# Gates' operations, low parts of the rotary weights and value weights moved in a fused attention and expert kernel

## The chip, the cores and the metric

The kernel runs on one core of a Trainium2 chip, as one program. The metric is the time of one execution on the device in microseconds, the lower the better. Five engines run their own instruction streams and meet at semaphores: PE (matrix products), DVE (VectorE), ACT (ScalarE), POOL (GpSimd) and SP, which here only issues DMA transfers. The rows call TensorE's weight loads PEld and the queues in which an engine issues transfers SPq and ACTq.

## The reference

A transformer block with modulation from a condition vector, attention with low-rank queries, keys and values and rotary parts, and a routed mixture of experts. Inputs: x of 4 x 512 x 256, 16 heads.

```
mod = (silu(c) @ wmod)                       # sa, ca, ga, sb, cb, gb
ga = (2*(ga >= 0) - 1) * max(|ga|, 0.25)      # the gates
gb = (2*(gb >= 0) - 1) * max(|gb|, 0.25)
h  = layernorm(x) * (1 + ca) + sa
c_q, c_kv = rmsnorm(h @ Wq_down), rmsnorm(h @ Wkv_down)
q, k, v   = c_q @ Wq_up, c_kv @ Wk_up, c_kv @ Wv_up
q_rope, k_rope = rope(h @ Wq_rope), rope(h @ Wk_rope)
attn = softmax((q k^T + q_rope k_rope^T) * scale)
x = x + ga * (attn @ v) @ Wout
h = layernorm(x) * (1 + cb) + sb
x = x + gb * (experts(h) + shared(h))         # 16 experts, 4 of them for each token
```

## The kernel before, in words

Float32 products are made of three: every operand is split in a high and a low part (`wr_hi`/`wr_lo`, `qk[..., 0/1, :]`, `mout[:, 0/1]`), and `mm3` (lines 677 to 679) multiplies high by high, high by low and low by high. ScalarE writes the high part, VectorE subtracts it from the source for the low part, and TensorE waits for both.

The work has four stages: inputs and latents, a passage up to attention, the attention loop, the experts. The change touches the second and the third.

The attention loop has 256 units: a head of a batch is four units, one for each tile of 128 keys, a pair of heads is eight, a batch 64. In unit u TensorE weighs values (`weigh_values`, line 857), forms the scores of unit u + 3 (`score`), the products for the maximum of unit u + 9 (`score_max`, line 834) and what `AUX_AT[u]` lists: rotary rows of a pair (`pr`), latent rows (`kl`), turned outputs (`ot`, line 811), the output product (`op`). ScalarE takes two exponentials for each unit (lines 1631, 1634), GpSimd the low part `p_lo` (line 1896), `rotate` (line 1874) and `add_rows`. VectorE's list in a unit is fixed: `turn` (lines 1216, 1217), `low_outputs`, `gated`, `row_max` (line 1243, nine units ahead, two PSUM banks), then `safe_gate` in units 4 to 19, `low_rows` (line 1223), and in every fourth unit `normalise` (lines 1250, 1253). Each engine works through its own list in order.

`safe_gate(b, step)` (lines 1262 to 1268) makes ga and gb of batch b from the raw gates in `gate[:, b + 1]`, 128 x 512 floats, in four chained operations. Its scratch is `y_gate`, where `gated` later writes the product of gates and output.

`shift_row(s)` on SP (line 560) copies a head's four rows of maxima to row 0 of `qk` for the scores of that head; `pad_slots(b)` on ScalarE's queue (line 1674) writes constant rows to the `slots` in HBM, 2880 KB for a batch, at unit 12 of the batch.

Ahead of the loop: line 1190 makes `wr_lo`, the low part of all rotary weights, 8 pairs of heads, in one VectorE operation of 4096 elements, and `wr_l` tells it. It stands between `norm_latents(0)` and `split_latents(0)`, `squares(1)`. `squares(1)` feeds GpSimd's `inverse_norms(1)` (line 1859, `rms`), that `norm_latents(1)` (lines 1137, 1139). Then come the turns of pair 1 behind the fills of `rows_f` (SP, lines 537 and 543), four low rows, the value weights `mout` (TensorE line 870, ScalarE 1692, VectorE 1201, two PSUM banks used in turn, four quarters), eight maxima, and the turns of pair 2. The raw gates are TensorE products (`row_modulations`, line 757, two banks in turn) that ScalarE copies (`row_gates`, line 1592). `wr_raw` and the value weights' source `wout_s` lie in the memory of `qk`, whose first writers wait for that reason on `wr_l` and `m_mm`.

The functions that the diff touches, and what calls them:

Of the kernel before, what the change touches and what calls it, by code (L numbers as in the profile page):

```python
# [39 lines left out]
TB = SEQ // P  # L40
# [83 lines left out]
GATES_AT = 4  # L124
# [13 lines left out]
def program(nc, x, cT, wmod, wdn, wqup, wkup, wvup, wout, wrope, trig, eye, qnw_bc, kvw, kvw2, wgate, w13, w2,  # L138
            route, out):
    ctx = ExitStack()  # L140
    with ctx:
# [141 lines left out]
        gabs, gsgn = (y_gate[:, n].rearrange("p q d -> p (q d)") for n in range(2))  # L283
# [214 lines left out]
        def _(sp):  # L498
# [47 lines left out]
            def fill_latents(s):  # L546

                b = s // H
                if s < RING:
                    sp.wait_ge(*((m_mm, 4) if s >= 2 else (wr_l, 1)))  # L550
                else:
                    sp.wait_ge(s_score, TB * (s - RING + 1))
                sp.dma_start(qk[SPARE:RD, s % RING, 0].bitcast(F32), lat_st[KL:LATENTS, b % 2].bitcast(F32))\
                    .then_inc(q_lat[s % RING], 16)
# [120 lines left out]
        def _(pe):  # L675
# [186 lines left out]
            def value_weights():  # L862
                pe.wait_ge(ld_v, 48)
                pe.wait_ge(p_dnev, NB)
                for q in range(4):
                    if q >= 2:
                        pe.wait_ge(m_ev, q - 1)
                    for pr in range(2 * q, 2 * q + 2):
                        for s in range(2):
                            mm = pe.matmul(out_bank[q % 2][s * KL:(s + 1) * KL, (pr % 2) * D:(pr % 2 + 1) * D],  # L870
                                           wvup_s[:, 2 * pr + s, :], wout_s[:, 2 * pr + s, :], start=True, stop=True)
                    mm.then_inc(m_mm, 1)
# [16 lines left out]
            row_modulations(1)  # L889
            aux(("kl", 1))  # L890
            value_weights()
            row_modulations(2)
            pe.wait_ge(p_clo, NB)
            pe.wait_ge(spared, 2)
            for k in range(TB):
                score_max(k)
            row_modulations(3)
            for k in range(TB, 2 * TB):
                score_max(k)
# [181 lines left out]
        def _(dve):  # L1081
# [82 lines left out]
            def up_weights():  # L1164
                dve.wait_ge(ld_c, 16 * 4)
                for z in range(2):
# [22 lines left out]
            dve.wait_ge(wr_h, 1)  # L1189
            dve.tensor_tensor(wr_lo[:].rearrange("p k g n -> p (k g n)"), wr_raw,  # L1190
                              wr_hi[:].bitcast(F32).rearrange("p k g n -> p (k g n)"), ALU.subtract).then_inc(wr_l, 1)
# [3 lines left out]
            def value_weights():  # L1195

                for q in range(4):
# [59 lines left out]
            def safe_gate(b, step):  # L1257

                g = gate[:, b + 1].rearrange("p w n -> p (w n)")
                if step == 0:  # L1260
                    dve.wait_ge(g_ev, b + 1)
                    dve.tensor_scalar(gsgn, g, 0.0, 0.5, ALU.is_ge, ALU.subtract)
                elif step == 1:
                    chain(dve.scalar_tensor_tensor(out=gabs, in0=g, scalar=-1.0, in1=g, op0=ALU.mult, op1=ALU.max))
                elif step == 2:
                    chain(dve.tensor_scalar(gabs, gabs, 0.25, 2.0, ALU.max, ALU.mult))
                else:
                    chain(dve.tensor_tensor(g, gabs, gsgn, ALU.mult))
# [4 lines left out]
            split_latents(1)  # L1273
            split_latents(2)
# [3 lines left out]
            for s in range(2):  # L1278
                low_rows(s, 1)
                low_rows(s, 0)  # L1280
            value_weights()
# [25 lines left out]
            for u in range(UNITS):  # L1307
# [10 lines left out]
                if GATES_AT <= u < GATES_AT + 4 * NB:  # L1318
                    safe_gate((u - GATES_AT) // 4, (u - GATES_AT) % 4)
# [252 lines left out]
        def _(act):  # L1572
# [111 lines left out]
            act.wait_ge(wr_l, 1)  # L1684
# [5 lines left out]
            for q in range(4):  # L1690
                act.wait_ge(m_mm, q + 1)
                act.activation(mout[:, 0, 2 * q:2 * q + 2, :], out_bank[q % 2][:].rearrange("p (a n) -> p a n", a=2),
                               ACT.Copy, scale=kvw2_s[:, 0:1]).then_inc(m_h, 1)
            row_gates(2)
            row_gates(3)
# [127 lines left out]
        def _(pool):  # L1823
# [80 lines left out]
            pool.wait_ge(wr_l, 1)  # L1904
# [151 lines left out]
```

## Time and profile before

| | us |
|---|---|
| median of 3 runs | 1024.6 (1023.91 to 1026.63) |
| profiled execution | 1026.2 |
| its span | 1024.4 |
| PE busy | 876.5 (86%) |
| DVE busy | 733.5 (72%) |
| POOL busy | 675.8 (66%) |
| ACT busy | 573.9 (56%) |
| TensorE clock granted, mean | 0.927 of full |

Busy time is the sum over instructions and overlaps a little where an engine pipelines. A stretch in which one engine is busy all the time is bound by it; elsewhere the waits have to be read. The span is that of the profiled execution, and the rows date everything from its start.

### The profile page before, as it was taken

The page shows a single profiled execution, that of the slowest core. Times are in us where ns is not written, and L with a number is a line of the kernel's source. Part 1 is how long each engine was busy: PE and PEld are TensorE (multiplying, and loading weights), DVE is VectorE, ACT ScalarE, POOL GpSimd, SP SyncE. Part 2 cuts the span into 40 slices and gives each one's busy share as a digit, 9 for nine tenths or more (in the row PEclk, how much of TensorE's full clock was granted, in tenths as well). Part 3 has the DMA queues.
Part 4 walks back from the last instruction along what each step waited for, and adds up shares of the span by engine and source line. Part 5 has one row for each costly group of instructions (what it writes and reads, how often), then busy time and mean ns, then how long its engine had stood idle before and what let it go on. Part 6 is the DMA issues. An engine that isn't in the chain of part 4 may idle for free.

```text
span 1024.4 us, 19916 instructions
## 1 busy us (share of the span) xinstructions
PE 876.5 (86%) x6996; PEld 744.5 (73%) x6996; DVE 733.5 (72%) x1596; ACT 573.9 (56%) x1071; POOL 675.8 (66%) x641
## 2 busy tenths in 40 slices
PE   5678889999999999999999988449974999999920
PEld 5546568888878888788887877438853899999910
DVE  5766997878887788786879775664843566666656
ACT  1335667788787877887787876422310444444400
POOL 3664667888888788887887975505675355555544
PEclk9889989999999999999999998858996899999965
DMA  7561421333523235232325253323222333333264
GB/s 289 195 155 34 148 44 40 81 79 80 155 44 85 55 85 174 48 81 48 85 54 155 48 205 113 100 51 114 88 106 107 109 115 122 116 120 119 82 236 174
DMA packets 65757, 111.20 MB, mean 109 GB/s; under 512 B 16918, under 2 KB 43293, under 8 KB 63821
## 3 DMA queue, kind: packets, MB, share of 16 engines
q1 hardware_dynamic: 46905, 69.24, 25.3%
q10 hardware_dynamic: 11843, 22.84, 6.3%
q0 software_dynamic: 6912, 17.84, 4.5%
q8 instruction: 59, 0.97, 0.4%
q14 instruction: 38, 0.30, 0.1%
HBM read 46.06 MB, written 39.58 MB: 84 GB/s over the span
## 4 chain that ended last, share of the span: by engine, by line
PE 60%; DVE 12%; DMA 9%; POOL 9%; issue 6%; ACT 3%; SPq 0%; POOLq 0%; DVEq 0%; ACTq 0%
PE bank L677 13%; PE bank L679 11%; PE bank L678 11%; PE bank L857 7%; DMA slots<-h,slot_i 7%; PE bank L1072 7%; PE bank L834 4%; POOL p_lo L1896 3%; POOL slots L1951 2%; PE bank L1044 2%; PE bank L931 2%; DVE nmax L1243 2%; POOL turns L1874 1%; DVE turns L1216 1%; POOL h_hl L1852 1%
## 5 line engine op out<-in xcount | busy, mean ns | idle before, releaser
L1896 POOL TENSOR_TENSOR p_lo<-p_f,p_hi 128x512 f16<-128x512 f32 x256 | 326.4, 1286 | 57.3 <-ACT p_f L1634 56.8
L1243 DVE TENSOR_REDUCE nmax<-bank 128x1 fp32r<-128x512 f32 x256 | 174.6, 686 | 96.2 <-PE bank L834 92.6
L1631 ACT ACTIVATE p_hi<-bank,log_up 128x512 f16<-128x512 f32 x256 | 176.2, 688 | 114.4 <-PE bank L679 105.5
L1634 ACT ACTIVATE p_f<-bank,log_up 128x512 f32<-128x512 f32 x256 | 175.3, 685 | 11.3 <-POOL p_lo L1896 11.3
L857 PEld LDWEIGHTS bank<-vals,p_hi 128*128 128x128 f16 x2048 | 111.1, 98 | 54.2 <-issue 27.0
L857 PE MATMUL bank<-vals,p_hi 128*128 128x66 f16 x2048 | 139.6, 195 | 10.1 <-POOL p_lo L1896 9.6
L1874 POOL TENSOR_TENSOR turns<-turns 128x512 f32<-128x512 f32 x64 | 90.8, 1420 | 66.9 <-DVE turns L1217 66.9
L1223 DVE TENSOR_TENSOR qk<-rows_f,qk 128x512 fp32r<-128x512 f32 (+1 forms) x128 | 131.9, 1030 | 2.2
L677 PE MATMUL bank<-qk 128*128 128x512 f32 x256 | 123.4, 482 | 11.1 <-issue 10.2
L857 PE MATMUL bank<-vals,p_lo 128*128 128x66 f16 x1024 | 121.8, 194 | 0.0
L834 PE MATMUL bank<-qk 128*128 128x512 f32 x256 | 104.6, 410 | 3.7 <-DVE nmax L1243 3.6
L1951 POOL DMA_INDIRECT slots<-h,slot_i x64 | 66.1, 1033 | 57.9 <-DMA slots<-h,slot_i 24.5
L679 PE MATMUL bank<-qk 128*128 128x512 f32 x256 | 103.3, 404 | 0.0
L678 PE MATMUL bank<-qk 128*128 128x512 f32 x256 | 101.8, 398 | 0.0
L857 PEld LDWEIGHTS bank<-vals,p_lo 128*128 128x128 f16 x1024 | 96.8, 97 | 0.5
L834 PEld LDWEIGHTS bank<-qk 128*128 128x128 f32 x256 | 79.3, 310 | 17.9 <-DVE nmax L1243 6.8
L1964 POOL DMA_INDIRECT parts<-h,sel_i x80 | 79.8, 997 | 13.2 <-POOL idle L1963 11.9
L1072 PE MATMUL bank<-w_p,gT 88*128 x320 | 82.2, 379 | 0.0
L1623 ACT ACTIVATE qk<-rows_f 128x512 fp32r<-128x512 f32 (+1 forms) x128 | 80.6, 629 | 1.9 <-DMA rows_f<-turns 0.3
L1963 POOL TENSOR_TENSOR idle<-mhalf 128x1 f32<-128x1 f32 x80 | 14.9, 186 | 83.6 <-ACT h L1817 83.5
L1817 ACT ACTIVATE h<-bank 128x256 f32<-128x256 f32 x80 | 30.8, 385 | 61.3 <-PE bank L1072 61.3
L1528 DVE TENSOR_TENSOR x_hl<-bank,x_hl 128x256 fp32r<-128x256 f32 x80 | 34.0, 425 | 40.3 <-ACT x_hl L1804 40.0
(229 smaller groups left out, 2133.2 us busy)
## 6 DMA issues: line engine op xcount, KB each, us to landing
rows_f<-turns SPq DMA_DIRECT2D x64, 256.0 KB, 3.9
slots<-pad ACTq DMA_DIRECT2D x4, 2880.0 KB, 10.1
h<-slots SPq DMA_DIRECT2D x80, 144.0 KB
w_hi<-parts SPq DMA_DIRECT2D x16, 512.0 KB, 8.5
rows_f<-kl_f SPq DMA_DIRECT2D x32, 192.0 KB, 3.0
w_raw<-in_w ACTq DMA_DIRECT2D x4, 1408.0 KB, 11.8
h_dram<-h_hl SPq DMA_DIRECT2D x3, 1024.0 KB, 3.9
qk<-lat_st SPq DMA_DIRECT2D x16, 192.0 KB, 4.0
```

What stands on the lines that cost most here:

```text
L677: pe.matmul(dst, l_hi, r_hi, start=start, stop=False)
L678: pe.matmul(dst, l_hi, r_lo, start=False, stop=False)
L679: return pe.matmul(dst, l_lo, r_hi, start=False, stop=stop)
L834: pe.matmul(max_bank[q % 2][:], qk[:, s % RING, 0, 0, :].rearrange("k (p t) -> k t p", t=TB)[:, q, :], qk[:, s % RING, 1, 0, :], start=Tru ...
L857: mm = pe.matmul(out_bank[s % 2][:, q * VW:(q + 1) * VW], p[:, c, tok], vals[:, s // H * TB + c, a, :], start=(c == 0 and q == 0 and n == ...
L1072: mm = pe.matmul(y_bank[j % 2][:, 0:D], gT[:, j % 2, 0, h, :], w2_s[:, bass.ds(expert, 1), h, :].rearrange("p a n -> p (a n)"), start=(h = ...
L1223: dve.tensor_tensor(qk[rows, s % RING, x, 1, :], rows_f[rows, (s // 2) % 2, x, s % 2, :], qk[rows, s % RING, x, 0, :].bitcast(F32), ALU.su ...
L1243: dve.tensor_reduce(nmax[:, k % MAXES:k % MAXES + 1], max_bank[q % 2][:], AX_X, ALU.max, negate=True)\
L1631: act.activation(p_hi[:, u % TB, :], score_bank[u % 2][:], ACT.Exp, bias=log_up[:, 0:1], scale=SCALE)
L1634: act.activation(p_f[:, u % 2, :], score_bank[u % 2][:], ACT.Exp, bias=log_up[:, 0:1], scale=SCALE)\
L1874: pool.tensor_tensor(turns[:, 0, w], turns[:, 0, w], turns[:, 1, w], ALU.add if w else ALU.subtract).then_inc(s_eo, 1)
L1896: pool.tensor_tensor(p_lo[:, u % TB, :], p_f[:, u % 2, :], p_hi[:, u % TB, :], ALU.subtract).then_inc(s_pl, 1)
```

## The change

The gates' sixteen steps leave units 4 to 19 for units 4, 7, 10, ..., 49. Their scratch becomes `small` (`gate[:, 0]`) and the four operations are others: max(-g, g); max with 0.25; (g >= 0) times that; twice that less the magnitude. `wr_lo` is made in two goes: pairs 0 and 1 where all of it was made, pairs 2 to 7 behind `split_latents(1)`; `wr_l` counts to 2. Those that need only pairs 0 and 1 wait for 1, the others for 2. The value weights go in two halves, on TensorE with the products for the gates of batch 3 between them and those of batch 2 before `kl` of pair 1, on VectorE each half ahead of a head's low rows. The maxima follow in one row. ScalarE copies the gates of batch 2 ahead of `high_rows` and those of batch 3 between the halves.

```diff
-GATES_AT = 4
...
-        gabs, gsgn = (y_gate[:, n].rearrange("p q d -> p (q d)") for n in range(2))
...
-                    sp.wait_ge(*((m_mm, 4) if s >= 2 else (wr_l, 1)))
+                    sp.wait_ge(*((m_mm, 4) if s >= 2 else (wr_l, 2)))
...
-            def value_weights():
+            def value_weights(half):
                 pe.wait_ge(ld_v, 48)
                 pe.wait_ge(p_dnev, NB)
-                for q in range(4):
+                for q in (2 * half, 2 * half + 1):
                     if q >= 2:
                         pe.wait_ge(m_ev, q - 1)
...
             row_modulations(1)
+            row_modulations(2)
             aux(("kl", 1))
-            value_weights()
-            row_modulations(2)
+            value_weights(0)
+            row_modulations(3)
+            value_weights(1)
             pe.wait_ge(p_clo, NB)
             pe.wait_ge(spared, 2)
-            for k in range(TB):
+            for k in range(2 * TB):
                 score_max(k)
-            row_modulations(3)
-            for k in range(TB, 2 * TB):
-                score_max(k)
+            pe.wait_ge(wr_l, 2)
             aux(("pr", 0, 2))
...
-            dve.wait_ge(wr_h, 1)
-            dve.tensor_tensor(wr_lo[:].rearrange("p k g n -> p (k g n)"), wr_raw,
-                              wr_hi[:].bitcast(F32).rearrange("p k g n -> p (k g n)"), ALU.subtract).then_inc(wr_l, 1)
+            def low_rotary(at):
+                dve.wait_ge(wr_h, 1)
+                dve.tensor_tensor(wr_lo[:, :, at], wr_raw.rearrange("p (k g n) -> p k g n", k=KD, g=PAIRS)[:, :, at],
+                                  wr_hi[:, :, at].bitcast(F32), ALU.subtract).then_inc(wr_l, 1)
+
+            low_rotary(slice(0, 2))
             split_latents(0)
             squares(1)
...
                 if step == 0:
                     dve.wait_ge(g_ev, b + 1)
-                    dve.tensor_scalar(gsgn, g, 0.0, 0.5, ALU.is_ge, ALU.subtract)
+                    ins = dve.scalar_tensor_tensor(out=small, in0=g, scalar=-1.0, in1=g, op0=ALU.mult, op1=ALU.max)
                 elif step == 1:
-                    chain(dve.scalar_tensor_tensor(out=gabs, in0=g, scalar=-1.0, in1=g, op0=ALU.mult, op1=ALU.max))
+                    ins = dve.tensor_scalar(small, small, 0.25, None, ALU.max)
                 elif step == 2:
-                    chain(dve.tensor_scalar(gabs, gabs, 0.25, 2.0, ALU.max, ALU.mult))
+                    ins = dve.scalar_tensor_tensor(out=g, in0=g, scalar=0.0, in1=small, op0=ALU.is_ge, op1=ALU.mult)
                 else:
-                    chain(dve.tensor_tensor(g, gabs, gsgn, ALU.mult))
+                    ins = dve.scalar_tensor_tensor(out=g, in0=g, scalar=2.0, in1=small, op0=ALU.mult, op1=ALU.subtract)
+                chain(ins)
...
             split_latents(1)
+            low_rotary(slice(2, PAIRS))
             split_latents(2)
...
             for s in range(2):
+                value_weights(s)
                 low_rows(s, 1)
                 low_rows(s, 0)
-            value_weights()
...
-                if GATES_AT <= u < GATES_AT + 4 * NB:
-                    safe_gate((u - GATES_AT) // 4, (u - GATES_AT) % 4)
+                if u >= 4 and u % 3 == 1 and u // 3 <= 4 * NB:
+                    safe_gate((u // 3 - 1) // 4, (u // 3 - 1) % 4)
...
             row_gates(1)
-            act.wait_ge(wr_l, 1)
+            row_gates(2)
+            act.wait_ge(wr_l, 2)
...
             for q in range(4):
+                if q == 2:
+                    row_gates(3)
                 act.wait_ge(m_mm, q + 1)
...
-            row_gates(2)
-            row_gates(3)
...
             pool.wait_ge(wr_h, 1)
-            pool.wait_ge(wr_l, 1)
+            pool.wait_ge(wr_l, 2)
```

## Rows read from the trace of the kernel before

**Rows 1.** Timeline, VectorE, units 3, 19, 35, 51: start, duration, engine, line, operation.
```profile
102.98 0.42 DVE L1253 TENSOR_TENSOR o_tok<-bank,rinv 128x256 f32<-128x256 f32 x1
...
145.92 0.42 DVE L1253 TENSOR_TENSOR o_tok<-bank,rinv 128x256 f32<-128x256 f32 x1
...
180.69 0.42 DVE L1253 TENSOR_TENSOR o_tok<-bank,rinv 128x256 f32<-128x256 f32 x1
...
213.94 0.42 DVE L1253 TENSOR_TENSOR o_tok<-bank,rinv 128x256 f32<-128x256 f32 x1
```

**Rows 2.** Busy times by stretch: PE, PEld, DVE, ACT, POOL, clock, DMA share, GB/s.
```profile
103.00:145.90 42.90, 36.48 (x312) 27.77 (x311) 41.66 (x57) 29.38 (x48) 28.05 (x21) 0.92 0.36 104
...
123.60:135.30 11.70, 10.04 (x65) 8.06 (x65) 11.00 (x15) 6.38 (x11) 7.62 (x6) 0.71 0.40 115
...
164.20:197.40 33.20, 33.14 (x319) 27.63 (x318) 27.10 (x44) 26.62 (x44) 28.07 (x23) 1.00 0.30 77
```

**Rows 3.** Groups of VectorE by line, 103 to 146 us: busy us, mean ns.
```profile
L1262 DVE TENSOR_SCALAR y_gate<-gate 128x512 f32<-128x512 f32 x4 | 4.7, 1180 | 0.0
L1264 DVE SCALAR_TENSOR_TENSOR y_gate<-gate 128x512 f32<-128x512 f32 x4 | 3.5, 884 | 0.0
L1268 DVE TENSOR_TENSOR gate<-y_gate 128x512 f32<-128x512 f32 x4 | 3.1, 783 | 0.1
L1266 DVE TENSOR_SCALAR y_gate<-y_gate 128x512 f32<-128x512 f32 x4 | 2.8, 693 | 0.0
```

**Rows 4.** Timeline around TensorE's longest idle time in that stretch; in brackets idle time before.
```profile
117.13 0.40 ACTq L1674 DMA_DIRECT2D slots<-pad  x1
...
119.40 0.49 SPq L560 DMA_DIRECT2D qk<-nmax  x1
...
125.26 0.77 PE L677 MATMUL bank<-qk 128*128 128x512 f32 x1 [4.36 <-issue]
...
126.25 0.63 PE L679 MATMUL bank<-qk 128*128 128x512 f32 x1
```

**Rows 5.** Timeline: TensorE's first weighing of values.
```profile
92.04 0.19 PE L857 MATMUL bank<-vals,p_hi 128*128 128x66 f16 x1 [2.12 <-POOL p_lo L1896]
```

**Rows 6.** Timeline, TensorE: first and last product of an output group, a rotary product.
```profile
186.68 0.28 PE L677 MATMUL bank<-mout,oT 128*128 128x256 f32 x1
...
188.00 0.28 PE L679 MATMUL bank<-mout,oT 128*128 128x256 f32 x1
...
189.76 0.39 PE L678 MATMUL bank<-h_st,wr_hi 128*128 128x512 f32 x1
```

**Rows 7.** Timeline around the low part of the rotary weights, 33 to 54 us.
```profile
33.66 2.37 POOL L1852 TENSOR_TENSOR h_hl<-h_f,h_hl 128x1024 fp32r<-128x1024 f32 x1 [5.18 <-ACT h_hl L1579]
...
41.53 4.41 DVE L1190 TENSOR_TENSOR wr_lo<-qk_raw,wr_hi 128x4096 fp32r<-128x4096 f32 x1
...
42.19 7.61 POOL L1852 TENSOR_TENSOR h_hl<-h_f,h_hl 128x1024 fp32r<-128x1024 f32 x1 [2.64 <-ACT h_hl L1579]
...
50.42 2.90 POOL L1859 TENSOR_TENSOR rms<-ve,mhalf 128x16 f32<-128x16 f32 x1
```

**Rows 8.** Timeline from the turns of pair 1 to the maxima, 62 to 84 us.
```profile
62.47 0.69 DVE L1216 TENSOR_TENSOR turns<-bank,trig_s 128x512 f32<-128x512 f32 x1 [1.05 <-DMA rows_f<-turns]
62.55 2.59 ACT L1623 ACTIVATE qk<-rows_f 128x512 fp32r<-128x512 f32 x4 [0.29 <-DMA rows_f<-turns]
...
64.87 4.76 DVE L1223 TENSOR_TENSOR qk<-rows_f,qk 128x512 fp32r<-128x512 f32 x4
...
70.46 3.68 PE L870 MATMUL bank<-qk_raw,wvup_s 128*64 128x256 f32 x16 [3.80 <-DVE mout L1201]
...
77.17 2.70 DVE L1243 TENSOR_REDUCE nmax<-bank 128x1 fp32r<-128x512 f32 x4 [1.44 <-PE bank L834]
...
78.97 1.89 PE L757 MATMUL bank<-wmod_s,csil_bc 128*128 128x256 f32 x8
...
81.15 2.70 DVE L1243 TENSOR_REDUCE nmax<-bank 128x1 fp32r<-128x512 f32 x4 [1.28 <-PE bank L834]
```

More of the change, by code:

```diff
@@ L1188, in _, with value_weights @@
                 .then_inc(ab_l, 1)
-            dve.wait_ge(wr_h, 1)
-            dve.tensor_tensor(wr_lo[:].rearrange("p k g n -> p (k g n)"), wr_raw,
-                              wr_hi[:].bitcast(F32).rearrange("p k g n -> p (k g n)"), ALU.subtract).then_inc(wr_l, 1)
+            def low_rotary(at):
[3 more added lines that the diff above has]
+            low_rotary(slice(0, 2))
             split_latents(0)
             squares(1)
-            def value_weights():
-                for q in range(4):
+            def value_weights(half):
+                for q in (2 * half, 2 * half + 1):
                     dve.wait_ge(m_mm, q + 1)
```

## The prediction, made before the changed kernel was run

> **What bounds the kernel now.** I read the granted clock and busy times by stretch first, then the normalisation of each head as a clock of the attention loop, then the engines around its start.
>
> The loop runs 256 units. `normalise` runs once in four, so its rows date the units: unit 3 at 102.98, unit 19 at 145.92, unit 35 at 180.69, unit 51 at 213.94 [rows 1]. Sixteen units thus take 42.94 us, 34.77 and 33.25. In a 33.20 us stretch of the steady part PE is busy for 33.14 at clock 1.00, with DVE at 27.10 and POOL at 28.07 [rows 2]: PE sets the pace. In the first stretch it is DVE: busy 41.66 of 42.90 [rows 2]. What is there and not later is `safe_gate`, four operations for each of four batches in units 4 to 19: 4.7 + 3.5 + 3.1 + 2.8 = 14.1 us [rows 3]. PE also stands still there for 4.36 us, until 125.26: the score of head 4 needs the row of maxima that SP sent off at 119.40, 2.3 us after ScalarE had put the 2880 KB `pad` transfer on the DMA engines [rows 4].
>
> Ahead of the loop, up to the first weighing of values at 92.04 [rows 5], PE works in short bursts between waits; who ends each wait is the chain that I follow below.
>
> **Part 1, the gates.** Removed from units 4 to 19: 14.1 us of DVE. Put back: steps at units 4, 7, ... 49, of which six (4 to 19) stay in the first block, five come in units 20 to 35 and five up to 49. The forms change: three two-input operations and one single-operand one for each batch. Their prices are the rows' means, 884 and 783 ns for two inputs, 693 for the two-constant scalar form [rows 3]; I take 0.85 for each, so 5.1 us in the first block. DVE's other work in 16 units is 27.10 in the steady part [rows 2], less what the first block does not have yet: two `gated` and one `low_outputs`, 0.7 each by their size, so 25.0. DVE then needs 30.1 us. PE needs the steady 33.2 less the output products, which start at unit 23: two groups of twelve, from 186.68 to 188.00 plus one spacing of 0.12, 1.44 each [rows 6], and less one turn of outputs, 0.5: 29.8. Two engines at 29.8 and 30.1, coupled through two banks of maxima, do not run at the larger of the two: that is the lower bound. The upper is the old block less only the operations taken out, 42.94 - (14.1 - 5.1) = 33.9. I take 31.8, halfway, since the gate is now one unit in three and DVE can catch up between. Gain: 42.94 - 31.8 = 11.1 us (9.0 to 12.8, and 7 if the new steps are stretched by POOL to the rows' longest). The 4.36 us stall is inside it: if DVE no longer lags, row 4's maxima leave before the pad transfer. If it lags still, up to 4.4 of the 11.1 is lost.
>
> Units 20 to 35: five steps add 4.3 to 27.1, 31.4 under PE's 33.2. The block took 34.77, partly PE coming back from a low clock; I take 34.1, gain 0.6 (-1.0 to 1.5). Units 36 to 51: DVE 31.4 again, POOL 28.1 plus what the gates hold it up; PE goes on at 33.25 with small slips, -0.3 (-1.5 to 0). Nothing else reads the scratch (`small`) before unit 107. Sum of part 1: 11.4 us.
>
> POOL's p_lo shares something with DVE: POOL's subtraction of one input took 2.37 us beside no long DVE operation and 7.61 beside the rotary low part of 4.41 us [rows 7]. So each gate step may hold POOL for up to its own length: 5.3 x 0.7 = 3.7 on 28.07 in a block, 31.8 of 33.2.
> The Trainium skill (SBUF — State Buffer, "Who interferes with whom") says that a VectorE instruction with two SBUF inputs, or one in a two-port mode, and a GpSimd instruction that reads SBUF exclude each other for a whole instruction. The 7.61 agrees. By that rule all four new forms lock the pair, as all four old ones did, and spreading them moves the blocking into blocks where POOL also adds rows; that speaks against the change and is rival B below. The same section says that a GpSimd instruction which only writes SBUF is not held; no row here has the new overlap of that kind.
>
> **Part 2, the rotary low part in two goes.** The whole is 4096 elements in 4.41 us [rows 7]; a quarter, 1.1, now stands ahead of `split_latents(0)` and `squares(1)`, and 3.3 go behind `split_latents(1)`. So DVE reaches `squares(1)` 3.3 us earlier, though not before ScalarE's high part of the latents; POOL's subtraction (start 42.19) is free of the long operation and ends at 45 to 46.5 instead of 49.8; the power `rms` starts at 47.1 instead of 50.42 [rows 7]. Taken: 3.3 us (2.5 to 3.9), carried to `norm_latents(1)`, ScalarE's `kl_f`, SP's fills of `rows_f`, and the first of the DVE's turns of pair 1, 62.47 to 59.2 [rows 8]. The 3.3 us moved back fit where DVE stood idle: 2.9 us before the latents of batch 2 and 1.05 before that turn, the latter noted in its row [rows 8]. If they do not fit, 0.5 is lost. What now waits for both goes (SP's first latents, ScalarE's `high_rows`, POOL's zeroing and, behind it, rotate(1)) gets them at about 57.3, before its other inputs.
>
> **Part 3, the order ahead of attention.** In the old order DVE did all four low rows (64.87, 4.76 us) before the value weights, PE's third quarter of value weights could start only at 70.46 after 3.80 us idle, and the maxima came in two groups, 77.17 to 79.87 and 81.15 to 83.85, with the gates' products of batch 3 (1.89 us) between [rows 8]. New, by the same durations:
> ScalarE's `row_gates(2)` now stands ahead of `high_rows`. Its products follow PE's turn of the latents at 55.4 to 56.3 by two groups of 1.89, so end at 60.0; the copy ends at 60.7, which is 1.5 later than the fills: a new wait, with four `high_rows` (2.59), `key_latents(1)` and two copies of value weights queued behind it. These end at 63.3, 63.9, 64.6 and 65.2. DVE, done with its turns at 61.7, waits for them, does two low parts to 66.0 and low rows of head 0 to 67.5. PE does the first half of the value weights at 61.3 to 63.2, the products of batch 3 to 65.1, and the second half to 67.2 by 0.66 us after each bank is free. ScalarE's copies end at 67.9, DVE's low parts at 68.9, low rows of head 1 at 70.4. Eight maxima in one chain, 0.60 to 0.65 each, end at 75.4 instead of 83.85: 8.45 us earlier. From there to 92.04 the order is the old one (scaled values' low part, turns of pair 2, POOL's rotations, low probabilities), so the loop starts at about 83.7. I take 8.3 (5 to 10.5); parts 2 and 3 are in this one number, since the 3.3 is carried through the 1.5 lost.
>
> **Sum.** 8.3 + 11.4 = 19.7 us. The profiled execution took 1026.2 (span 1024.4 and 1.8 around it), so it would take 1006.5. It lies 1.6 over the median of the three runs, 1024.6, so the median would be 1004.9; I say 1005. Nothing behind the loop depends on absolute time, so the shift is carried whole.
>
> **The rivals.**
> A, the forecast: 1005, own range 1000 to 1010; 0.62.
> B, DVE and POOL stay at their limit while gates run: the six steps in the first block are worth less than hoped, the maxima's DMA still falls behind the pads (4.4), and the ten later steps cost PE 0.4 each, half a step. For it: POOL at 28.07 and PE at 33.14 of 33.2 leave little play. Against: DVE had 6 us idle in the steady 33.2. Part 1 then brings 11.4 - 4.4 - 4.0 = 3.0: 1024.6 - 8.3 - 3.0 = 1013.3; 0.15.
> C, the start brings only part 2, less the new wait: a fill, ScalarE's queue or a PE at 1.2 GHz (granted clock 0.71 in one stretch after a stall [rows 2]) takes the place of the reordered waits. Then 3.3 - 1.5 = 1.8 for the start and 11.4 for the gates: 1024.6 - 13.2 = 1011.4; 0.16.
> D, slower than before: denser waits with DVE and PE at equal load, PE falls to its lower level after each stall and stays there. A 512-column matmul has 0.63 us there against 0.39 [rows 4, 6], that is 1.6 times, so each us of full-clock PE work costs 0.6 more; the gain of 19.7 is gone once 33 us of such work (one block) runs low. Two blocks: 63 x 0.6 = 38, 1024.6 - 19.7 + 38 = 1043. Against: from unit 35 on PE ran at 1.00. 0.03.
> E, B and C together with more of each, so that nothing can be told from before: the products wait on ScalarE anyway and the gates merely smear; 1023; 0.04. This is also the case that the order in the text is not the order that decides.
>
> One run of this kernel cannot tell less than about 0.3%, 3.1 us, from no change. Faster: A, B and C, 0.93. Same: 0.04. Slower: 0.03. Range: from 999, where both parts give the upper ends of their terms (11.1 to 12.8, 0.6 to 1.5, -0.3 to 0, 8.3 to 10.5: 24.8), to 1014, which takes in the middles of B and C and leaves out D and E.
>
> **What would show it.** The first normalisation (102.98) at 94 to 95; from it to that of unit 19 31 to 33 us; no PE idle over 2 us around the pad transfer; POOL's last input subtraction under 4.5 us; the last of the first eight maxima at about 75; blocks of units 20 to 51 at 33.2 to 34.5. The prediction is wrong if DVE is still busy for over 95% of the first block with over 35 us, if the loop starts later than 87, or if the steady blocks after unit 51 are not at 33.2.

## The result, and the profile after

The changed kernel takes 1016.16 us (median of 11 runs) against 1026.2 of the kernel before in 11 runs beside it: ratio 0.9908, 95% interval 0.9883 to 0.9932. It is 9.4 us faster (7.0 to 12.0); 19.7 had been forecast, and the time lies above the range. The spans of the two profiled executions differ by 12.5 us, 1011.9 against 1024.4. Of the kernels below, the profiled execution of e1 was in a slower state that adds 31 us behind the loop and nothing to its dates in the loop.

First what dates the loop, the first weighing of values and the normalisations of units 3, 19, 35 and 51, in the timeline of the changed kernel (start, duration, engine, line, operation).

```profile
86.47 0.19 PE L855 MATMUL bank<-vals,p_hi 128*128 128x66 f16 x1 [2.00 <-POOL p_lo L1900]
...
95.90 0.42 DVE L1254 TENSOR_TENSOR o_tok<-bank,rinv 128x256 f32<-128x256 f32 x1
...
129.48 0.42 DVE L1254 TENSOR_TENSOR o_tok<-bank,rinv 128x256 f32<-128x256 f32 x1
...
166.17 0.42 DVE L1254 TENSOR_TENSOR o_tok<-bank,rinv 128x256 f32<-128x256 f32 x1
...
202.08 0.42 DVE L1254 TENSOR_TENSOR o_tok<-bank,rinv 128x256 f32<-128x256 f32 x1
```

Against [rows 5] and [rows 1]: the loop starts 5.57 us earlier; units 3 to 19 take 33.58 instead of 42.94; units 19 to 35 take 36.69 instead of 34.77, and 35 to 51 take 35.91 instead of 33.25. From unit 51 to unit 227 the blocks are alike. So the change gains at the start and in the first block, and gives part of it back in the two blocks into which it moved ten of the sixteen steps.

The same blocks by engine (length, PE, PEld, DVE, ACT, POOL, granted clock, DMA share, GB/s) and, for units 19 to 51, whom TensorE waited for.

```profile
95.90:129.50 33.60, 31.82 (x306) 24.87 (x305) 31.69 (x48) 26.67 (x44) 28.29 (x21) 1.00 0.46 132
129.50:166.20 36.70, 34.59 (x323) 28.05 (x322) 34.60 (x50) 27.74 (x46) 30.21 (x22) 1.00 0.21 43
166.20:202.10 35.90, 34.08 (x320) 27.67 (x319) 34.48 (x50) 26.96 (x45) 30.80 (x22) 1.00 0.33 83
```

```profile
PE bank L855 <- POOL p_lo L1900: 3.4, 4, 1.0
```

VectorE had been put at 31.4 us for each of these blocks; it is busy for 34.6 and 34.5. Its list by line in units 19 to 35 says why. The first line is `low_rows` in the changed kernel, the second the same operations in e3, a kernel without the steps.

```profile
L1224 DVE TENSOR_TENSOR qk<-rows_f,qk 128x512 fp32r<-128x512 f32 (+1 forms) x8 | 10.2, 1274 | 0.2
...
L1224 DVE TENSOR_TENSOR qk<-rows_f,qk 128x512 fp32r<-128x512 f32 (+1 forms) x8 | 7.6, 953 | 0.1
```

The eight `low_rows` are 0.32 us longer each, 2.6 us together. The five steps take 1.06 us each in the mean (681 to 1565 ns), where the prediction had 0.85.

How one step reaches TensorE, from the timeline around unit 19:

```profile
128.62 0.60 DVE L1265 TENSOR_SCALAR gate<-gate 128x512 f32<-128x512 f32 x1
...
130.42 0.68 DVE L1218 TENSOR_TENSOR turns<-bank,trig_s 128x512 f32<-128x512 f32 x1
...
131.18 1.29 POOL L1878 TENSOR_TENSOR turns<-turns 128x512 f32<-128x512 f32 x1 [2.23 <-DVE turns L1218]
132.44 4.30 POOL L1900 TENSOR_TENSOR p_lo<-p_f,p_hi 128x512 f16<-128x512 f32 x3
...
134.09 0.20 PE L855 MATMUL bank<-vals,p_hi 128*128 128x66 f16 x1 [1.01 <-POOL p_lo L1900]
```

The step stands ahead of the normalisation and the second half of the turns. GpSimd's rotation is next in its queue and waits 2.23 us for those turns, with three low parts of probabilities behind it; then TensorE waits 1.01 us for the first of these. In e3, without steps, GpSimd waits at this place as well, but for 1.54 us, and TensorE waits for nothing in these two blocks; in the changed kernel it is 2.23 or 2.71 us. So the step lengthens a wait at the head of GpSimd's queue, and TensorE's idle time comes from what stands behind it. This idle time, 3.4 us for the low parts and 0.3 for turns, is not all: the two blocks are 6.1 us longer than in e3, and the rest is in TensorE's busy time (68.7 us against 66.3), whose cause was not read.

The start, in the lines that answer to [rows 7] and [rows 8]:

```profile
41.43 1.21 DVE L1189 TENSOR_TENSOR wr_lo<-qk_raw,wr_hi 128x1024 fp32r<-128x1024 f32 x1
...
42.08 2.81 POOL L1856 TENSOR_TENSOR h_hl<-h_f,h_hl 128x1024 fp32r<-128x1024 f32 x1 [2.63 <-ACT h_hl L1582]
...
47.65 2.90 POOL L1863 TENSOR_TENSOR rms<-ve,mhalf 128x16 f32<-128x16 f32 x1
...
54.40 3.34 DVE L1189 TENSOR_TENSOR wr_lo<-qk_raw,wr_hi 128x3072 fp32r<-128x3072 f32 x1
...
60.10 0.69 DVE L1217 TENSOR_TENSOR turns<-bank,trig_s 128x512 f32<-128x512 f32 x1 [1.16 <-DMA rows_f<-turns]
...
71.03 2.89 DVE L1244 TENSOR_REDUCE nmax<-bank 128x1 fp32r<-128x512 f32 x4
...
71.77 2.29 PE L832 MATMUL bank<-qk 128*128 128x512 f32 x3 [2.90 <-DVE nmax L1244]
```

The pads and the row of maxima of head 4, which answer to [rows 4]. The row now leaves 0.45 us ahead of the pads, as forecast, and TensorE does not wait for it.

```profile
108.57 0.49 SPq L558 DMA_DIRECT2D qk<-nmax  x1
...
109.02 0.40 ACTq L1677 DMA_DIRECT2D slots<-pad  x1
```

### The profile page after: what moved, and what is told of

Its sections match the earlier page's. It is cut to its first block, busy times and chain, and to the rows that moved or that the text cites. A ratio compares the mean times of both kernels' runs of the same rounds, so it can differ in the third digit from the quotient of the medians.

```text
span 1011.9 us, 19921 instructions
## 1 busy us (share of the span) xinstructions
PE 871.3 (86%) x6996; PEld 738.7 (73%) x6996; DVE 737.5 (73%) x1597; ACT 573.9 (57%) x1071; POOL 675.1 (67%) x641
## 4 chain that ended last, share of the span: by engine, by line
PE 57%; DVE 12%; DMA 10%; POOL 10%; issue 6%; ACT 3%; SPq 0%; POOLq 0%; ACTq 0%; DVEq 0%
PE bank L675 12%; PE bank L677 10%; PE bank L676 10%; DMA slots<-h,slot_i 8%; PE bank L855 7%; PE bank L1070 7%; POOL p_lo L1900 5%; PE bank L832 4%; POOL turns L1878 2%; PE bank L1042 2%; PE bank L929 2%; DVE nmax L1244 2%; DVE qk L1224 1%; DVE turns L1218 1%; DVE h L1567 1%
## 5 line engine op out<-in xcount | busy, mean ns | idle before, releaser
L1900 POOL TENSOR_TENSOR p_lo<-p_f,p_hi 128x512 f16<-128x512 f32 x256 | 329.9, 1301 | 46.0 <-ACT p_f L1637 45.1
L1637 ACT ACTIVATE p_f<-bank,log_up 128x512 f32<-128x512 f32 x256 | 175.4, 685 | 14.8 <-POOL p_lo L1900 14.7
L832 PEld LDWEIGHTS bank<-qk 128*128 128x128 f32 x256 | 79.2, 310 | 18.7 <-DVE nmax L1244 7.4
```

The lines of the kernel that those rows point to most:

```text
L832: pe.matmul(max_bank[q % 2][:], qk[:, s % RING, 0, 0, :].rearrange("k (p t) -> k t p", t=TB)[:, q, :], qk[:, s % RING, 1, 0, :], start=Tru ...
L1637: act.activation(p_f[:, u % 2, :], score_bank[u % 2][:], ACT.Exp, bias=log_up[:, 0:1], scale=SCALE)\
L1900: pool.tensor_tensor(p_lo[:, u % TB, :], p_f[:, u % 2, :], p_hi[:, u % TB, :], ALU.subtract).then_inc(s_pl, 1)
```

## The experiments

The stage dates of all kernels, read from the same rows (first weighing; normalisation of unit 3; then the lengths of blocks of 16 units), with the ratio to the kernel before where the kernel was timed in rounds. A block repeats to 0.2 us from kernel to kernel where nothing in it is changed, except for single drops of the clock of 1.5 us, of which the last section tells (and except for e16's 33.55 from unit 51 on).

The first weighing does not repeat so well. Nine kernels have the whole start of the changed one (changed, e1, e3, e5, e11, e14, e15, e18, e19), and it comes at 85.51 to 87.54, 86.4 in the mean; three have the old start (before, e2, e10), and it comes at 90.74 to 92.04, 91.6 in the mean. Each is one profile. So a difference of two single first weighings tells little below 2 us.

| kernel | weighing | unit 3 | 3-19 | 19-35 | 35-51 | 51-67 | span | ratio (interval) |
|---|---|---|---|---|---|---|---|---|
| before | 92.04 | 102.98 | 42.94 | 34.77 | 33.25 | 33.19 | 1024.4 | |
| changed | 86.47 | 95.90 | 33.58 | 36.69 | 35.91 | 33.22 | 1011.9 | 0.9908 (0.9883-0.9932) |
| e1 start only | 86.46 | 95.85 | 42.95 | 34.75 | 33.22 | 33.23 | 1048.9 | 0.9939 (0.9915-0.9963) |
| e2 gates only | 90.74 | 101.70 | 33.57 | 36.71 | 36.08 | 33.23 | 1018.2 | 0.9967 (0.9942-0.9991) |
| e3 no steps | 87.54 | 98.50 | 32.55 | 33.25 | 33.22 | 33.23 | 1011.8 | 0.9810 (0.9779-0.9841) |
| e4 idle units | 87.11 | 96.44 | 35.85 | 33.86 | 34.68 | 34.94 | 1017.9 | 0.9921 (0.9889-0.9953) |
| e5 reduces | 86.18 | 95.58 | 32.55 | 35.97 | 34.80 | 33.23 | 1011.9 | 0.9877 (0.9841-0.9913) |
| e6 one go | 91.01 | 101.96 | 33.58 | 36.68 | 35.91 | 33.18 | 1014.9 | 0.9938 (0.9919-0.9958) |
| e7 gates 2 back | 86.98 | 96.37 | 33.58 | 36.65 | 35.90 | 33.23 | 1011.9 | 0.9894 (0.9874-0.9915) |
| e9 start early | 83.45 | 92.86 | 33.57 | 36.68 | 36.11 | 33.17 | 1012.1 | 0.9892 (0.9854-0.9931) |
| e10 pads later | 92.02 | 101.41 | 42.09 | 33.23 | 33.21 | 33.24 | 1021.8 | 0.9991 (0.9968-1.0013) |
| e11 three ops | 86.76 | 96.16 | 32.24 | 33.90 | 33.85 | 33.19 | 1007.9 | 0.9851 (0.9827-0.9875) |
| e12 both | 82.61 | 92.02 | 32.25 | 33.89 | 33.88 | 33.19 | 1001.6 | 0.9816 (0.9791-0.9840) |
| e13 scores early | 82.13 | 91.54 | 32.26 | 33.87 | 33.86 | 33.24 | 1002.7 | 0.9787 (0.9770-0.9804) |
| e14 four ops, unit 0 of 4 | 85.66 | 95.05 | 32.38 | 33.88 | 33.88 | 33.86 | 1006.2 | 0.9844 (0.9819-0.9868) |
| e15 three ops, every third | 87.08 | 98.04 | 33.59 | 36.67 | 33.24 | 33.19 | 1012.9 | one run |
| e16 TensorE filled | 85.70 | 96.64 | 33.58 | 36.64 | 35.90 | 33.55 | 1012.8 | one run |
| e17 split only | 88.01 | 97.41 | 43.00 | 33.21 | 33.22 | 33.23 | 1014.4 | one run |
| e18 unit 1 of 4 | 85.51 | 94.92 | 34.06 | 35.47 | 35.46 | 35.46 | 1009.6 | one run |
| e19 unit 3 of 4 | 85.99 | 95.38 | 33.20 | 34.97 | 34.93 | 34.94 | 1009.5 | one run |

**e1 and e2, the change taken apart.** e1 is the changed kernel with `GATES_AT`, the old scratch and the old `safe_gate`; e2 is the kernel before with only the gates' part of the diff.

> The changed start (rotary low parts in two goes, value weights, gates' products, maxima) with the old gates, four operations a batch in units 4 to 19. Theory T (the changed kernel's loss in units 20 to 51 is the price of the gates' steps there): unit 3 at about 96, units 3 to 19 again near 42 us, units 20 to 51 at 67 to 68 us as before, span 7 us under the kernel before, so about 1017. Rival P (the new start leaves the engines in another phase, and that costs units 20 to 51): these units take 71 to 73 us here too, and the span is only 2 to 4 us shorter.

> The start of before with the changed gates in units 4, 7, ... 49. Theory T: unit 3 at 103, units 3 to 19 in 33 to 34 us, units 20 to 51 in 72 to 73 us, a gain of 5 us in all, so span about 1019. Rival P: units 20 to 51 at 67 to 69 us, gain 9 to 10 us, span about 1015. The two single changes should add up to the 12.5 us of the profiled pair under T.

The two parts do not act on each other: e1 has the start of the changed kernel and the loop of before, e2 the loop of the changed one to 0.2 us in each block. Their gains by the ratios, 6.3 and 3.4 us, add up to about 9.6, and the changed kernel gains 9.4. P falls: 71 to 73 us in units 19 to 51 come with the new steps (72.79) and not with the new start (67.97).

**e3, e4, e5: what a step costs.**

```diff
 # e3
-                if u >= 4 and u % 3 == 1 and u // 3 <= 4 * NB:
-                    safe_gate((u // 3 - 1) // 4, (u // 3 - 1) % 4)
 # e4
+GATE_UNITS = [0, 8, 9, 16, 24, 25, 32, 40, 41, 48, 56, 57, 64, 72, 73, 88]
...
+                if u in GATE_UNITS:
+                    safe_gate(GATE_UNITS.index(u) // 4, GATE_UNITS.index(u) % 4)
 # e5, for all four operations
+                ins = dve.tensor_reduce(small[:, 4 * b + step:4 * b + step + 1], g, AX_X, ALU.max)
```

> The changed kernel with none of the sixteen steps (the gates stay raw, the floor at 0.25 is left out). The output product starts later than unit 20, so units 3 to 19 have a floor of 29.8 us by TensorE's own matmuls. Theory T: 30 to 31 us there and 66.5 to 67 us for units 20 to 51, so the steps cost 9 to 10 us in the changed kernel and the span falls to about 1002. Rival P: units 20 to 51 stay above 70. Rival S (something else than the gates, the start itself, holds the first block): units 3 to 19 stay above 32.

> The changed kernel with its sixteen steps in units 0, 8, 9, 16, 24, 25, 32, 40, 41, 48, 56, 57, 64, 72, 73, 88: those in which VectorE stood idle for 1.1 to 1.5 us in the steady part. Theory T with its second half (a step costs what it delays the turns of the next pair, and with them GpSimd's rotations): steps in these units cost 0.1 to 0.3 us each instead of 0.6, units 3 to 19 take 30.5 to 31.5, all sixteen cost under 4 us, span about 1005. Rival L (a step costs by the exclusion of GpSimd alone, wherever it sits): 0.6 each still, span 1010 to 1012.

> The changed kernel in which each of the sixteen steps is a tensor_reduce over the same 512 columns of the gates (the gates are not computed): as long on VectorE as a step without company (0.68 us), but with one SBUF input. Its units are the same, 4, 7, ... 49. Theory L (a step costs because it and GpSimd's subtractions keep each other off, which delays low_rows, turns and p_lo): the steps become nearly free, units 3 to 19 about 31 us, units 20 to 51 about 67 us, span about 1003. Rival V (a step costs its time on VectorE): as in the changed kernel less the stretching, units 3 to 19 at 33 and units 20 to 51 at 71 us.

e3 leaves the sixteen steps out, and e5 puts a maximum over the same columns in place of each, so both compute other gates. Without steps units 19 to 51 take 66.47 us, with them 72.60: ten steps cost 6.1 us, where the prediction had them nearly free. The first block takes 32.55, not 30 to 31, and is only 1.0 shorter than with six steps. But in 1.6 of it TensorE waits for a row of maxima, which it does not in the changed kernel; with this taken off the block would take 30.9. By this estimate its floor is 30.9 and not 29.8, and the six steps cost 2.6. S had the block above 32, which came, but not by the start. e3's profiled span, 1011.8, is not at the 1002 of T: its last normalisation is 4.8 us before that of the changed kernel, but what lies behind it took 380.3 us and not 375.6. By the ratios e3 is 10 us under the changed kernel.

e4 went against both of its theories: the first two blocks after 19 are cheaper by 4 us, but the price goes on to unit 99 and TensorE waits 3.47 us for the maxima in the first block; it is no gain (that choice of units is explained below).

e5 is between L and V: ten operations with one SBUF input cost 4.3 us instead of 6.1, and they take 0.67 to 0.69 us each on VectorE and are never stretched. By this one comparison, in these units, the mutual exclusion of VectorE and GpSimd is about a third of the price, and the time in VectorE's list two thirds.

**e11, e14, e15, e18, e19: number or place.** e11 makes f = max(|g|, 0.25) x sign in three operations; the others vary only the units.

```diff
 # e11, e15
+                    ins = dve.tensor_scalar(small, g, 0.0, 0.5, ALU.is_ge, ALU.subtract)
...
+                    ins = dve.scalar_tensor_tensor(out=g, in0=small, scalar=4.0, in1=g, op0=ALU.mult, op1=ALU.mult)
...
+                    ins = dve.scalar_tensor_tensor(out=g, in0=g, scalar=0.5, in1=small, op0=ALU.max, op1=ALU.mult)
 # e11: u % 4 == 0 (4 to 48); e15: u % 3 == 1 (4 to 37)
 # e14: four operations, u % 4 == 0 (4 to 64); e18: u % 4 == 1; e19: u % 4 == 3
```

> The changed kernel with three operations a batch instead of four (sign as +-0.5; twice the magnitude as 4 x sign x gate; its maximum with 0.5 times the sign), in units 4, 8, ... 48. Both theories of a step's price give 12 of 16 of it, since each step still has 512 columns and two of three have two SBUF inputs: by the sixteen steps' 8.8 us that is 2.2 less, units 3 to 19 at 32.5 to 33.5, units 20 to 51 at 70.5 to 71.5, span about 1010. Rival (a step costs by how it meets the turns; units divisible by 4 meet the normalisation never and the turns never): half of it, 4 us less.

> The changed kernel with its four operations a batch in units 4, 8, ... 64. Theory U (the unit decides: every third unit meets the units of the turns and of head ends, every fourth does not): 0.2 us a step as in the three-operation kernel, units 3 to 19 at 32.3, 19 to 51 at 67.8, 51 to 67 at 34, all sixteen under 4 us, span about 1007.5. Rival F (number and form decide): the costs of the changed kernel, 0.55 each, 8.8 in all, spread to unit 64, span 1011 to 1012.

> The changed kernel with three operations a batch in units 4, 7, ... 37. Theory U: units 3 to 19 at 33.6 (six steps, as in the changed kernel), 19 to 35 at 36.7, 35 to 51 at 34. Rival F: 32.3, 34.5, 33.5.

> The changed kernel with its sixteen steps in units 5, 9, ... 65, each ahead of a low_rows of two SBUF inputs. Theory U1 (a step is cheap only where nothing else but the maximum stands in the unit): 0.5 us or more each, units 19 to 35 at 35.2 or more instead of 33.9. Rival U2 (only the units of the turns are dear): as with units divisible by four, 33.9.

> The changed kernel with its sixteen steps in units 7, 11, ... 67, ahead of the normalisation and, in every second of them, of half the turns. Theory U1: 0.5 us or more each. Rival U2: the four of every sixteen units cost more than in any other place, 36 or more for units 19 to 35, as GpSimd's rotation waits for the turns.

The place decides. Four operations in units divisible by 4 give 33.88 for a block with four steps, 0.16 us a step over e3's 33.25; three operations in every third unit give 36.67, as the changed kernel. In unit 1 of four a step costs 0.56, in unit 3 it costs 0.43 (U1 had said 0.5 or more); every third unit goes through all four places, with 0.69 a step in units 19 to 35 and 0.54 in 35 to 51. Unit 2, in which `low_rows` and every second time `low_outputs` stand, was not run by itself; that it is the dearest, about 1 us, is an estimate from these numbers. The prices do not simply add: e15's only step after unit 35 stands in unit 37, a unit 1 of four, and its block takes 33.24, as with none. Ahead of the step VectorE's list has only the maximum in unit 0, and behind it once in sixteen units a `gated`. F and U2 fall. e11's rival had the right direction and was too small: units 3 to 51 are 6.2 us shorter than in the changed kernel, where it had 4. e14 and e11 are faster than the changed kernel beyond both intervals.

The steps themselves are not shorter in e14: the four of a batch take 1.39, 0.74, 1.40 and 1.05 us in units 19 to 35. What is back near its old value is GpSimd's wait ahead of the rotation, 1.57 and 1.58 us. e4's list had five of its sixteen steps in unit 1, right behind another. Whom TensorE waited for in e14, units 19 to 51, to be set beside the 3.4 us above:

```profile
PE bank L855 <- POOL p_lo L1900: 0.6, 2, 0.4
```

**e10, the transfer of the pads.** In the kernel before, `pad_slots(0)` at unit 28 instead of 12.

> The kernel before, with the first batch's constant rows sent at unit 28 instead of 12 (the other batches as they were). Theory D (4.36 us of the old first block were the row of maxima waiting behind that transfer): units 3 to 19 take 38.5 us instead of 42.9, and what VectorE's own time made of the block is the rest. Rival: VectorE is late anyway and the stall only moves, 41.5 to 43.

D falls: of the stall of [rows 4] 0.5 us is left, and the block loses only 0.85 us of 42.94, since TensorE now waits 4.4 us for VectorE's maxima instead of 1.7. VectorE was late, which let the row fall behind the pads, and would have held TensorE anyway. (Units 19 to 35 are 1.5 shorter, by a clock drop less.)

**e6, e17, e7: the parts of the start.** e6 is the changed kernel with `low_rotary(slice(0, PAIRS))` alone, so in one go, and the waits set to 1, e17 the kernel before with only the two goes, e7 the changed kernel with `row_gates(2)` behind `high_rows(1, 0)`.

> The changed kernel with the rotary weights' low part in one operation again (4096 elements ahead of the split of the latents). By the prediction's step the split was worth 3.3 us (2.5 to 3.9), so the first weighing of values comes at 89.8 instead of 86.5. Rival: the chain behind it is held by something else, and it comes at 87 to 88. GpSimd's last input subtraction takes 7.6 us again instead of 2.8.

> The kernel before with the rotary low part in two goes and nothing else. By the changed kernel without the split (first weighing 91.0 against 86.5) the split is worth 4.5 us, by the prediction 3.3: first weighing at 87.5 to 88.7. If the two parts of the start do not add (both shorten the same wait), it is 86.5 to 87.5, and the new order alone gains nothing.

> The changed kernel with ScalarE's copy of batch 2's raw gates behind the four high_rows instead of ahead of them. The prediction held that this new wait cost 1.5 us. If so, ScalarE starts high_rows at about 60.2 with the fill (61.08 in the changed kernel), VectorE's value weights start 0.3 to 0.9 earlier and the first weighing comes at 85.6 to 86.2. Rival: VectorE and the two banks decide, and it stays at 86.5.

The table's first weighings would give the split 4.03 us alone (92.04 to 88.01) and 4.54 with the rest (91.01 to 86.47), and the new order 1.03 alone and 1.54 on top of it. But single first weighings differ by up to 2 us with nothing changed, so the parts are better read from dates nearer to them. From the start of the first rotary low part to the first turn of pair 1 it is 22.0 us in e6 and 18.4 to 18.7 in the nine kernels with the changed start, 3.4 to 3.6 less; the old starts have 20.9 (before) and 22.1 (e2, e10), e17 has 18.1. From that turn to the first weighing it is 27.1 to 29.6 us in the four kernels with the old order (before, e2, e10, e17: 28.5 in the mean) and 25.9 to 27.3 in the nine with the new one (26.4 in the mean). So the split is worth about 3.5 us, and the order about 2, with its size open by 1 to 2 us.

The wait for `row_gates(2)` that the prediction priced at 1.5 us shows in nothing: e7's first weighing comes 26.13 us behind that turn, which is within the nine.

**e16 and e9, the clock and the order behind the maxima.**

```diff
 # e16: fill(n) is n matmuls into the bank that pair 2 overwrites later
+            pe.wait_ge(*read_out(("pr", 1, 1)))
             for k in range(2):
                 score_max(k)
+            fill(12)
             for k in range(2, 2 * TB):
                 score_max(k)
+                fill(1)
 # e9: TensorE does pr of pair 2 between score_max(1) and (2); VectorE
+            turn(2, 0)      # between row_max(3) and row_max(4)
+            turn(2, 1)
```

> The changed kernel with eighteen extra rotary matmuls on TensorE whose results are overwritten: twelve behind the second maximum product and one behind each later one, so that it is not idle there. Theory C (the clock at 0.66 between 72 and 82 us is what makes the maxima and the products behind them late): clock 1.00 in that stretch, the maxima end 0.8 to 1.2 earlier, first weighing at 84.3 to 85.3 instead of 86.5. Rival: the clock falls in spite of it or VectorE holds the chain, and it stays at 86.4 to 87.

> The changed kernel with TensorE's rotary products of pair 2 between the second and the third maximum product (where it stood idle for 2.9 us and came back at the lower clock, 0.66 in the stretch behind), and VectorE's turns of pair 2 between the fourth and the fifth maximum. Theory C (the start missed its forecast by a drop of the clock and by the turns that stand behind all maxima): no idle time over 1 us in TensorE there, clock 1.00, first weighing at 80 to 82 instead of 86.5, span 5 us shorter. Rival W (another wait, on ScalarE's exponentials or the low part of the values, holds the loop): 85 to 86.

The clock of 72 to 82 us, changed kernel and e16:

```profile
72.00:82.00 10.00, 9.68 (x24) 6.03 (x24) 8.47 (x13) 1.26 (x3) 0.12 (x1) 0.66 0.02 0
```

```profile
72.00:82.00 10.00, 9.16 (x34) 6.15 (x33) 9.54 (x15) 2.72 (x5) 0.89 (x1) 1.00 0.09 11
```

With TensorE kept busy the clock stays at 1.00, and from the first maximum to the first weighing it takes 13.89 us (71.81 to 85.70) instead of 15.44 (71.03 to 86.47). The nine kernels with the changed start take 14.8 to 16.4 us for this, all with the same idle time of 2.9 us and a clock of 0.69 to 0.78 in the stretch, and the four with the old order had 1.00 there. So the lower level costs 1 to 2.5 us, 1.55 in this pair. That fits C. But nothing is won in the end: e16's first weighing lies within the nine, and the clock drops later, between the first weighing and unit 3 (0.88 in 82 to 96 us, 10.94 instead of 9.43).

e9's first weighing is at 83.45, 3.0 us before the changed kernel's and 2.1 before the earliest of the nine; e12, with the same start, has 82.61. That is order, and less than the 4.5 to 6.5 of its theory. TensorE still stands for 2.5 us and has a clock of 0.66 in 72 to 82 us, though the theory had no idle time over 1 us and a clock of 1.00; VectorE pauses for no more than 0.31 us from 65.6 to 80.5. In the whole time e9 shows no gain over the changed kernel, neither in the ratio nor in the span: its last normalisation is 2.7 us earlier, and what lies behind it took 378.5 us instead of 375.6.

**e12 and e13, the pieces together.** e12 is e9 with e11's gates; e13 puts `score(0)` and `score(1)` ahead of `score_max(6)`.

> The early start of the third round with the three operations: the two gains should add, first weighing at 83.4, loop as with three operations alone, so 5 us under the changed kernel in span, about 1007, and about 16 under the kernel before. Rival: the earlier start meets the first steps, and the gain is under 3.

> As the kernel with early start and three operations, and TensorE's first two scores ahead of the last two maximum products, since they need only the first head's maxima. Theory C (the exponentials of the first unit wait for the last maxima): first weighing at 81.5 to 82.5 instead of 83.4. Rival W (VectorE, busy from 65.6 to 82, sets the pace and the low part of the values is late instead): 83.4 or later.

In the dates both gains add: e12 has the start of e9 and the loop of e11. It came out better than forecast, with a span of 1001.6 us where 1007 had been expected. e13 takes 1002.68 us against 1024.39 beside it, ratio 0.9787 (0.9770 to 0.9804): 21.8 us faster than the kernel before, and beyond the changed kernel's interval. By the dates 19.3 of them are 9.9 us of start and 10.7 in the first block, less 1.3 paid in units 19 to 51, where the changed kernel pays 6.1; the other 2.5 were not placed. That e13 itself is better than e12 is not shown, since their intervals overlap; its first weighing is 0.48 us earlier, which is less than the nine differ by.

## Why the prediction was wrong

It had 19.7 us; what the profiles show of the change is 8.8, by the blocks: 5.6 at the first weighing, 9.4 in the first block, less 3.5 (36.69 against the 33.23 of e10, in which the old loop had no clock drop) and 2.7. That is the measured 9.4 within its interval. The profiled pair shows more since the execution of before had three clock drops of 1.5 us in the loop that the other had not.

**The step that failed** is "Units 20 to 35: five steps add 4.3 to 27.1, 31.4 under PE's 33.2", with the same for units 36 to 51 ("small slips"). It was forecast at +0.3 us together. Measured are -4.6 in the profiled pair (68.02 to 72.60), in which before had a clock drop, and -6.1 against e3. The sums were compared over 16 units, but VectorE's work is not spread over them: a unit of TensorE is 2 us, VectorE has 0.7 in unit 0 of four and up to 3.6 in a unit with turns. A step in a full unit pushes the turns, and GpSimd's rotation waits for them at the head of its queue with the low probabilities behind it. e14 shows that steps there are nearly free (0.16 each), as forecast, if they stand in the empty units.

The sum of 31.4 itself was short too, by 3.2 us. The prediction let the steps hold GpSimd up, and left out that GpSimd holds VectorE up: `low_rows` went from 953 to 1274 ns in the mean, 2.6 us in a block, and the steps took 1.06 us and not 0.85. e14 had steps of 1.14 us and `low_rows` of 1116 ns and paid only 0.6 us a block, so the longer operations alone are not the cause.

It was rival B, held at 0.15, that named the ten later steps; its price for them, 0.4 each, was 0.6. Of the 4.4 us that it took off the first block 1.7 came, and the maxima did not fall behind the pads.

The exclusion of VectorE and GpSimd did what [rows 7] had shown: GpSimd's input subtraction went from 7.61 to 2.81 us beside the shorter rotary operation. The new 3.34 us operation left GpSimd's zeroing, which only writes, at 1.80 us beside it, and 1.79 right behind it. The Trainium skill (SBUF — State Buffer, "Who interferes with whom") says that a VectorE instruction with two SBUF inputs contends with a GpSimd instruction that reads SBUF and not with one that only writes it; both numbers agree. As a price of the steps the exclusion is the smaller part (e5).

Inside the failed term 0.6 us was also credited for the old block's return from a low clock, as if it were a property of the kernel. It is not: e10 and e17 have the same steps in the block as before and 33.2 us.

**The first block**: 9.36 of 11.1. The forecast of 31.8 missed 33.58 by 1.8. By the estimate from e3 the floor is 30.9 and not 29.8, and the six steps cost 2.6 rather than 2. The stall went for the reason forecast, since the row of head 4 left before the pads.

**The start**: 5.57 of 8.3 in the profiled pair, 5.2 by the means of nine and three kernels. The split, taken at 3.3, is worth about 3.5: there the step was right, and the size too. In the profiled pair the first turn of pair 1 came only 2.4 us earlier (62.47 to 60.10), because before's was the earliest of the old ones. The order, at 5.0 (8.3 less 3.3), is worth about 2. Dated by the first turn of pair 1 the maxima end 17.0 us later (60.10 to 77.11) against 16.2 forecast and 20.5 in e17 (59.33 to 79.8): so 3.5 of that term were there. Against e17 it was lost on both sides. The fills landed 0.8 later. And behind the maxima TensorE, idle for 2.9 us because all maxima now wait for VectorE's last low rows, came back at the lower clock and did the maxima and the products of pair 2 in it; e16 prices that at 1 to 2.5 us. "From there to 92.04 the order is the old one" held for the order, and not for the clock: the old order had run at 1.00 there. The wait of 1.5 us that the forecast took off for `row_gates(2)` showed in nothing (e7).
Rival C named this (PE at 1.2 GHz in place of the reordered waits), but its price left 1.8 us for the whole start.

**What was right**: the gain in the first block with VectorE as its bound; 33.2 from unit 51 on; GpSimd's subtraction under 4.5 us; and, by luck in part, the first normalisation, forecast at 94 to 95 and measured at 95.90. The weighing ahead of it missed by 2.8 us, and a clock drop of 1.5 that before had between the two was not there. D did not happen. None of the three signs by which the prediction called itself wrong appeared (VectorE busy for over 35 us in the first block, a loop that starts after 87, other blocks than 33.2 after unit 51); what told of the miss were the blocks of units 20 to 51, which it had at 33.2 to 34.5.

## What to carry to other kernels

Work put into another engine's slack has to fit the slack of the unit in which it stands, not the sum over a period: list what each unit of the order already holds, and put the steps where only the pacing operation stands. Ask then which queue waits at its head for what comes behind the step. And when waits are reordered, look where the matrix engine now stands idle; what it gains in order it can lose in clock.

## What the runs showed of the hardware

- Where TensorE is busy nearly all the time, one drop of its clock cost 1.5 us, always nearly the same. Between the first weighing and unit 3 the kernels need either 9.3 to 9.4 us (clock 1.00 in this stretch) or 10.94 to 10.96 (clock 0.84), and the same program start gives both (e10 the first, before the second):

```profile
92.00:103.00 11.00, 10.96 (x91) 8.74 (x92) 5.62 (x10) 7.84 (x13) 7.17 (x6) 0.84 0.21 45
```

```profile
92.00:101.50 9.50, 9.48 (x91) 7.78 (x92) 5.68 (x10) 7.70 (x13) 7.22 (x6) 1.00 0.25 52
```

  Units 19 to 35 with the old gates take 33.2 or 34.8 likewise. Two profiles can so differ by a few such steps that no edit explains; blocks of a fixed count of units, compared over several kernels, show them for what they are.
- A 2 KB transfer that is issued while the 2880 KB one of the pads is under way lands late. The pads take 9.5 to 10.1 us from issue to landing in the first block. A row of maxima takes 1.9 us (median). In before it was issued 2.3 us behind the pads and took 5.8 us, and TensorE stood for 4.4 us [rows 4]. In e4 it was issued 1.0 us behind them and took 5.8 (3.5 us of idle time). In e3 the row of head 4 left ahead of the pads, but the next one still fell 2.3 us before they had landed and took 5.4 (1.6 us of idle time). In the changed kernel the one row left 0.45 us ahead of the pads and the next 0.26 us behind their landing: 1.9 and 2.6 us, and no idle time.
